# A perceiver layer on one core: tile 0 of the experts tied to expert 0, its weights fetched and split in earlier stages

## What is computed

```python
gout = x @ Wgate + bgate                      # 1024 tokens, 8 experts
topv, topi = jax.lax.top_k(gout, 2)
topw = jax.nn.softmax(topv, axis=-1)
x1 = x @ W1[e] + b1[e];  x2 = x @ W2[e] + b2[e];  z = x1 * x2
g = z @ Wg[e] + bg[e]
o = g * sigmoid(g) * (z @ Wl[e] + bl[e])
y = o @ W3[e] + b3[e]                         # summed over the token's two experts with topw
```

## Time and profile before

| | us |
|---|---|
| median of 3 runs (lowest, highest) | 2017.91 (2017.11, 2163.83) |
| profiled execution | 2020.24 |
| its span, first to last instruction | 2018.5 |
| mean granted TensorE clock, share of full speed | 0.961 |
| TensorE busy | 1843.3 (91%) |
| VectorE busy | 1601.7 (79%) |
| ScalarE busy | 1225.7 (61%) |

### The profile page before, as it was taken

The page is one execution under the profiler, slowest core; times in us unless marked ns, Lnnn a source line. Parts: engine busy times, 40 slices in busy tenths (PEclk is TensorE's granted clock), DMA queues, the critical chain, the costliest instruction groups (busy, mean ns, idle before and its releaser), DMA issues. The chain is left out here.

```text
span 2018.5 us, 33904 instructions
## 1 busy us (share of the span) xinstructions
PE 1843.3 (91%) x10010; PEld 1513.9 (75%) x10010; DVE 1601.7 (79%) x2790; ACT 1225.7 (61%) x2259; POOL 559.9 (28%) x388
## 2 busy tenths in 40 slices
PE   5978999999999999999999999999698756999995
PEld 4757777777777777777777777777485446999994
DVE  6758888898798988988889889878574856888863
ACT  3436666666676666766766767666452425777751
POOL 3022423334234232342342423412003731000003
PEclk9989999999999999999999999999798977999996
DMA  4621111111111111111111111010552026666632
GB/s 157 269 74 36 40 49 56 40 40 47 53 47 38 38 57 48 43 42 58 45 38 40 55 48 46 22 32 11 197 199 99 1 100 214 210 214 204 219 119 73
DMA packets 158260, 172.49 MB, mean 85 GB/s; under 512 B 13528, under 2 KB 124912, under 8 KB 158192
## 3 DMA queue, kind: packets, MB, share of 16 engines
q1 hardware_dynamic: 156656, 167.44, 25.6%
q0 software_dynamic: 1536, 4.20, 0.6%
HBM read 127.04 MB, written 44.56 MB: 85 GB/s over the span
## 5 line engine op out<-in xcount | busy, mean ns | idle before, releaser
L590 POOL TENSOR_TENSOR cl<-nrm,ch 128x255 fp32r<-128x255 f32 (+1 forms) x208 | 308.8, 1487 | 577.0 <-DVE ch L762 577.0
L688 ACT ACTIVATE s<-score 128x512 f32<-128x512 f32 (+1 forms) x416 | 248.4, 597 | 352.2 <-PE score L127 352.1
L721 DVE TENSOR_TENSOR s<-s,most 128x512 f32<-128x512 f32 (+1 forms) x416 | 321.9, 774 | 69.4 <-ACT most L664 69.4
L727 DVE TENSOR_TENSOR pl<-s,ph 128x512 fp32r<-128x512 f32 (+1 forms) x416 | 357.7, 860 | 0.7 <-ACT ph L670 0.7
L125 PE MATMUL acc<-ph,cl 128*128 128x512 f32 (+1 forms) x832 | 342.3, 411 | 1.4 <-DVE pl L727 1.4
L125 PE MATMUL score<-qsh,tl 128*128 128x512 f32 (+1 forms) x832 | 339.0, 407 | 0.8 <-DVE tl L756 0.8
L127 PE MATMUL score<-qsh,th 128*128 128x512 f32 (+1 forms) x832 | 326.7, 393 | 0.0
L126 PE MATMUL score<-qsl,th 128*128 128x512 f32 (+1 forms) x832 | 326.6, 393 | 0.0
L127 PE MATMUL acc<-ph,ch 128*128 128x512 f32 (+1 forms) x832 | 326.0, 392 | 0.0
L126 PE MATMUL acc<-pl,ch 128*128 128x512 f32 (+1 forms) x832 | 325.6, 391 | 0.0
L739 DVE TENSOR_TENSOR top<-top,s 128x512 f32<-128x512 f32 (+1 forms) x352 | 250.2, 711 | 19.4 <-ACT s L688 19.3
(11 more groups left out here) (257 smaller groups left out, 3456.6 us busy)
## 6 DMA issues: line engine op xcount, KB each, us to landing
raw<-in_ctx_in SPq DMA_DIRECT2D x192, 128.0 KB, 2.0
wr<-in_W SPq DMA_DIRECT2D x45, 512.0 KB, 4.8
queries_scratch<-stage SPq DMA_DIRECT2D x32, 512.0 KB, 3.5
qr<-queries_scratch SPq DMA_DIRECT2D x64, 256.0 KB, 3.3
outputs_scratch<-o SPq DMA_DIRECT2D x64, 256.0 KB, 2.4
at<-outputs_scratch SPq DMA_DIRECT2D x16, 1024.0 KB, 7.6
wr<-in_Wg SPq DMA_DIRECT2D x15, 1024.0 KB, 7.1
wr<-in_Wl SPq DMA_DIRECT2D x15, 1024.0 KB, 5.7
```

The costliest lines, as they stand in the source:

```text
L590: pool.tensor_tensor(cl[0:rows(t), t, 1:DIM], nrm[0:rows(t), t, 1:DIM], ch[0:rows(t), t, 1:DIM].bitcast(F32), ALU.subtract).then_inc(r_low, 1)
L688: act.activation(s[0:n, u, t, :], score[0:n, slot(0, u, t) % 2, :], ACT.Copy).then_inc(copied, 1)
L721: v.tensor_tensor(s[0:n, u, t, :], s[0:n, u, t, :], most[0:n, u, :], ALU.subtract).then_inc(shifted, 1)
L727: v.tensor_tensor(pl[0:n, ring(t), :], s[0:n, u, t, :], ph[0:n, ring(t), :].bitcast(F32), ALU.subtract).then_inc(p_low, 1)
```

## The change

Tile 0 is owned by expert 0 always: in `over`, the comparison for the first tile of expert 0 is with -1 instead of 0, so that it has a tile even with no tokens. With this its weights are known ahead of routing. A new class `Weights` holds the buffers and semaphores, and `load`, `high` and `low`. SP loads expert 0's weights at the end of its queue in `self_attention`. In `route`, ACT does `high` of all four parts first, and VectorE `low` of parts 0 and 1 behind the normalisation; parts 2 and 3 follow in `experts`. ACT and VectorE also split `xn` into `xnh` and `xnl` in `route`, which lie in the buffers `zh` and `zl`. The one-hot steps multiply these two parts in single passes into separate banks of `pp`, whose sums are copied as `xh` and `xl` without another subtraction. In `experts`, SP issues biases and weights of tile 1 ahead of the wait for `sent`. TensorE's order is `products(0)`, `gate(0)`, `first(1)`, and then steps from 0 with `gate(0)` left out. `y` lies in `xn` now, and `o` has a buffer of its own.

```diff
@@ self_attention, SP
                     sp.dma_start(flat[:, n * w4:(n + 1) * w4], nil[:, :]).then_inc(cleared, 16)
+                for n in range(4):
+                    ew.load(sp, *We, n, 0)
                 sp.wait_ge(cleared, 64)
@@ class Weights
+    def high(self, act, i, b, n):
+        act.wait_ge(self.w_in[n], (32 if n == 0 else 16) * (i + 1))
+        act.activation(self.wh[:, b, self.parts[n]], self.wr[:, self.parts[n]], ACT.Copy).then_inc(self.w_high[n], 1)
+
+    def low(self, v, i, b, n):
+        v.wait_ge(self.w_high[n], i + 1)
+        v.tensor_tensor(self.wl[:, b, self.parts[n]], self.wr[:, self.parts[n]],
+                        self.wh[:, b, self.parts[n]].bitcast(F32), ALU.subtract).then_inc(self.w_low[n], 1)
@@ route, ACT
+                for n in range(4):
+                    ew.high(act, 0, 0, n)
                 ln.scalar_copy(act)
+                act.activation(xnh[:, :, :], xn[:, :, :], ACT.Copy).then_inc(x_parts, 1)
@@ route, VectorE
                 ln.vector_normalise(v)
+                ew.low(v, 0, 0, 0)
+                ew.low(v, 0, 0, 1)
+                v.wait_ge(x_parts, 1)
+                v.tensor_tensor(xnl[:, :, :], xn[:, :, :], xnh[:, :, :].bitcast(F32), ALU.subtract
+                                ).then_inc(x_parted, 1)
...
-                for n in range(4):
+                inc(v.tensor_scalar(over[:, 0, 0:1], rank[:, TT, 0:1], -1.0, None, ALU.is_gt))
+                inc(v.tensor_scalar(over[:, 0, 1:], rank[:, TT, 1:], 0.0, None, ALU.is_gt))
+                for n in range(1, 4):
@@ experts, SP
-                e0 = expert(0)
+                first_biases(0, 0, 0)
+                gate_biases(0, 0, 0)
+                e1 = expert(1)
+                first_biases(1, 1, e1)
                 for n in range(4):
-                    weights(0, n, e0)
-                first_biases(0, 0, e0)
+                    weights(1, n, e1)
+                tile_rows(1, 1)
                 tiles(sp, step)
@@ experts, GpSimd
+                halves(0, 0, 0)
                 tiles(pool, step)
@@ experts, TensorE
+                pe.wait_ge(x_parted, 1)
                 for i in range(TT):
                     pe.wait_ge(hot_made, i + 1)
                     for c in range(DC):
-                        m = pe.matmul((pt, py)[c][:, 0, :], xn[:, i, c * P:(c + 1) * P], u[:, i % 2, :],
-                                      start=i == 0, stop=i == TT - 1)
+                        for n, w in enumerate((xnh, xnl)):
+                            m = pe.matmul(pp[:, 2 * c + n, 0, :], w[:, i, c * P:(c + 1) * P], hot_r[:, i % 2, :],
+                                          start=i == 0, stop=i == TT - 1)
                     m.then_inc(hot_used if i < TT - 1 else turned, 1)
+                pe.wait_ge(x_taken, 2)
+                products(0, 0)
+                gate(0, 0)
+                first(1, 1, 0)
                 tiles(pe, step)
@@ experts, ACT
-                high(0, 0, 0)
                 act.wait_ge(turned, 1)
-                act.activation(xh[:, 0, :], pt[:, 0, :], ACT.Copy).then_inc(x_half, 1)
-                act.activation(xh[:, 1, :], py[:, 0, :], ACT.Copy).then_inc(x_high, 1)
-                for n in range(1, 4):
-                    high(0, 0, n)
+                for c in range(DC):
+                    m = act.activation(xh[:, c, :], pp[:, 2 * c, 0, :], ACT.Copy)
+                m.then_inc(x_high, 1)
+                act.wait_ge(x_high, 1)
+                act.nop().then_inc(x_taken, 1)
+                x1_parts(0, 0, 0)
+                high_z(0, 0, 1)
+                high(1, 1, 0)
+                high(1, 1, 1)
+                gates(0, 0)
+                first(1)
                 tiles(act, step)
```

More of the change, by code:

```diff
@@ L1560, in weights @@
                 def weights(i, n, e):
[L1561 to L1567, removed]
+                    sp.wait_ge(w_low[n], i)
+                    ew.load(sp, *We, n, e)
                 def step(i, b, h):
@@ L1596, in _, with halves, step @@
                 pool.wait_ge(point5_made, 1)
+                def halves(i, b, h):
+                    if not on(i):
+                        return
+                    pool.wait_ge(bg_in[b], 16 * (h + 1))
+                    wait(pool, tanh_done, FC * (i - 1))
+                    pool.tensor_tensor(halfg[:, b], bias[:, b, 2 * FC:3 * FC], point5[:, :], ALU.mult
+                                       ).then_inc(b_half, 1)
+                def step(i, b, h):
+                    halves(i + 1, 1 - b, h if b == 0 else h + 1)
                 for i in range(TT):
@@ new lines, in gates @@
+                def gates(i, b):
+                    if not on(i):
+                        return
+                    for f in range(FC):
+                        act.wait_ge(g_made, FC * i + f + 1)
+                        if f == 0:
+                            act.wait_ge(b_half, i + 1)
+                        wait(act, u_done, FC * i + f - 1)
+                        act.activation(tanh[:, f % 2, :], pp[:, f, 0, :], ACT.Tanh, scale=0.5,
+                                       bias=halfg[:, b, f:f + 1]).then_inc(tanh_done, 1)
+                        act.activation(g[:, f % 2, :], pp[:, f, 0, :], ACT.Identity,
+                                       bias=bias[:, b, 2 * FC + f:2 * FC + f + 1]).then_inc(g_done, 1)
+                        if f == 2:
+                            high_o(i, 0)
@@ L1827, in step @@
                     low(i + 1, 1 - b, 2)
+                    low_z(i + 1, 1 - b, 1)
                     first(i + 2)
-                    low_z(i + 1, 1 - b, 1)
                     low(i + 2, b, 0)
                     low(i + 1, 1 - b, 3)
-                    if isinstance(i, int) and i == 0:
-                        v.wait_ge(sent, 16 * TT * TOP)
-                    for f in range(FC):
-                        gated(i, b, f)
-                        if f == 2:
-                            low_o(i, 0)
+                    if not isinstance(i, int) or i > 0:
+                        for f in range(FC):
+                            gated(i, b, f)
+                            if f == 2:
+                                low_o(i, 0)
@@ new lines, in _ @@
+                low(0, 0, 2)
+                v.wait_ge(turned, 1)
+                for c in range(DC):
+                    m = v.tensor_copy(xl[:, c, :], pp[:, 2 * c + 1, 0, :])
+                m.then_inc(x_low, 1)
+                v.wait_ge(x_low, 1)
+                v.nop().then_inc(x_taken, 1)
+                low(0, 0, 3)
+                for f in range(FC):
+                    product(0, 0, f)
+                    if f == 2:
+                        low_z(0, 0, 0)
+                low_z(0, 0, 1)
@@ L1852, in _ @@
+                low(1, 1, 0)
+                for f in range(FC):
+                    gated(0, 0, f)
+                    if f == 2:
+                        low_o(0, 0)
+                first(1)
                 tiles(v, step)
```

161 lines of the change are left out of this document (81 added, 80 removed).

## The result

The changed kernel takes 2028.73 us (median of 5 runs, 2028.1 to 2030.62) against 2020.59 us (5 runs) for the kernel before beside it on the same chip: ratio 1.0046, interval 1.0028 to 1.0064. One run of before took 2163.83 us in a slow state and is left out of the ratio; without it the median is 2019.25. The change costs some 9 us, by the interval 6 to 13; forecast were 7.7 us less. The profiled execution took 2030.62 us and spans 2028.9.

A forecast was written before the change was run, and what follows sets the result against it. TensorE runs expert tiles back to back from 1694 us, so only the stretch ahead can shrink: 9.0 us won at `products(2)`, less 1.3 for clock, gives 7.7 us and 2010.2 us; 8-in-10 range 2005 to 2015.5.

The forecast's parts named there:

- The step that failed: From the start of `products(2)` on: same matmul queue in both kernels, so the gain there lasts to the end.
- Clock: Experts' start: half-rate matmuls cost 1.3 us ahead of `products(0)` and 1.3 ahead of `products(2)`, nothing ahead of gate 0.
- the forecast's chain: Experts' start without clock losses: `products(0)` at 1658.8, gate 0 at 1667.15, `products(1)` at 1680.8, `products(2)` at 1694.6 us.
- What is late next: Ahead of `products(2)`: VectorE's 11.6 us chain sets its start 13.75 us after `products(1)`, TensorE idle some 8 us.
- Self-attention and route: Expert 0's weight fetch hidden, cost nothing; extra splits in route make it 0.2 us later, bounds 0 and 0.8.
- First rows in two parts: One-hot steps on split `xn`: `products(0)` starts at 1658.8 instead of 1660.83 us, gain 2.0, bounds 1.2 and 2.6.
- Arithmetic: Figures of 19.5 us idle time going, and of tile 1's rows landing at 1680.6 with scatters 2.4 later.
- The first (GpSimd held up): Scatters ahead of tile 1's rows: VectorE's two-input operations end them 2.4 us later, giving 2011.2 us; chance 0.12.
- The third (only the start is won, 2 to 4 us): Ahead of `products(2)`: `low` chain some 5 us longer, tile 2's transfer behind `sent` on SP; 2014 to 2016 us; chance 0.1.
- The slower case: Experts' start: scatters end so late that `x_in` and `b_half` come after the covered 11 us; 2020.5 us; chance 0.03.

The follow-up runs named there:

- e5: Changed kernel with 320 unused bytes ahead of the split weights and 192 behind them; 2015.66 us, ratio 0.9981 to the kernel before.
- e10: As e5, with 4, 6, 4 and 15 unread constant matmuls in TensorE's waits of the experts' start; 2010.97 us, 0.9954 to the kernel before.
- e13: Changed kernel with its own addresses, plus only the added constant matmuls of e10; 2024.15 us, ratio 1.0021 to the kernel before.
- e12: Changed kernel with 192 unused bytes behind the split weights; 2015.00 us, ratio 0.9975 to the kernel before.
- e2: Kernel before with 64 unused bytes ahead of `wh` and 64 behind `wl`; 2031.67 us, ratio 1.0054 to the unpadded kernel before.
- e3: Kernel before with 64 unused bytes behind `wl` alone; 2031.59 us, ratio 1.0057 to the unpadded kernel before.
- e1: Changed kernel with 64 unused bytes ahead of `wh` and 64 behind `wl`; 2022.59 us, ratio 1.0010 to the kernel before.
- e4: Changed kernel with 64 unused bytes behind `wl` alone; 2022.80 us, ratio 1.0006 to the kernel before.
- e7: As e5, plus pads of 64 bytes in the stages of queries, cross-attention and output projection; 2020.25 us, ratio 1.0001 to the kernel before.
- e9: As e5, plus 192 bytes ahead of the moving operands of cross-attention and its output projection; 2031.76 us, ratio 1.0063 to the kernel before.
- e11: As e5, but `gate(0)` back in its turn behind `products(1)` on all three engines; 2015.68 us, ratio 0.9985 to the kernel before.

## Why the prediction was wrong

Starts after that of `products(0)`, in us:

| | `gate(0)` | `products(1)` | `products(2)` | `gate(1)` |
|---|---|---|---|---|
| before | 33.1 | 25.8 | 44.1 | 52.6 |
| forecast for after | 8.4 | 22.0 | 35.8 | |
| after | 10.7 | 26.2 | 41.8 | 53.4 |
| e5 | 10.7 | 27.2 | 41.3 | 51.2 |
| e10 (clock kept) | 8.6 | 22.6 | 36.6 | 45.2 |

**The step that failed** is the sentence at the end of the first part: "From there both kernels have the same queue of matmuls, and what has been won at that point is won at the end, provided TensorE stays without a gap". It stayed without a gap and the queue is the same; its rate isn't. At `outputs(0)` the changed kernel was 1.5 us ahead, eleven tiles later 8.2 behind. By the ratios of after and e5 the term that I had at nothing is 0.0065 of the time, 13 us (by the two intervals, 9 to 18), of which 10 lie in the eleven tiles measured. It comes from the moved buffers, which stand in the diff and for which the forecast has no term. No wait, no busy share and no granted clock shows it.

**Clock.** I summed 1.3 ahead of `products(0)` and 1.3 ahead of `products(2)` and took the wait ahead of `gate(0)` as free. It wasn't (clock 0.62 from 1668 to 1671), nor was the 2.07 us ahead of `products(1)`, and the stretch from `products(2)` stayed at half rate until about 1706, 5.8 us and not 2.9. Keeping the clock gives 5 us by medians; at `gate(1)` it gives 6.0 with e5's addresses and 7.2 with the changed kernel's own (e13: 46.2). With it the forecast's chain, which stands in the table without its clock losses, holds to within 0.8 us at each of its three points. So the durations and their order in "What is late next" were right (a wait of 8 us, measured 7.7, ended by the last `low`), and the clock term was mis-sized: 2.6 forecast, 5 to 7 measured. The Trainium skill, "TensorE: Matmul & The Clock Gate", section "HAM oscillation — how this bites in real kernels", describes this: waits between short batches send the clock back each time, so that every batch starts slow. The trace of the kernel after agrees, for waits of 3.2 us and even 2.07; my forecast treated each wait by itself. In e5 the same wait of 2.07 us cost nothing, so the short one isn't a loss each time:

```profile
1688.00:1691.00 3.00, 3.00 (x27) 3.00 (x27) 0.96 (x2) 0.53 (x2) 0.00 (x0) 1.00 0.00 0
```

**Self-attention and route.** The issues for expert 0 hid, and `r_best` starts at 1636.65 us, against 1637.03 in the earlier trace rows. A shift of 0.2 us can't be told: in the other traces of the changed kernel that leave the stages ahead of `route` as they are, `r_best` starts anywhere from 1635.84 to 1638.98.

**First rows in two parts**: forecast 1658.8, measured 1658.64. That close a hit is luck, for the same reason; but from `r_best` to `products(0)` it is 22.0 us in after, e5, e10 and e12 alike, against 23.8 before, a gain of 1.8 as forecast.

**Arithmetic.** Two slips are in terms that the sum doesn't use: the idle time of the earlier trace rows is 18.8 us and not 19.5, and 1678.40 plus 2.4 is 1680.8, not 1680.6.

**Rivals.** The first (GpSimd held up) wasn't the cause: the last scatter starts at 1671.44 us, in the kernel before at 1671.36, and in e10 `products(1)` started at 22.6 us. The third (only the start is won, 2 to 4 us) is near the lead of 1.5 at `outputs(0)`, but for another reason than SP's queue: 3.0 of the 4.5 us won at `products(2)` are lost up to `outputs(0)`, most of them to the half rate. The slower case had a chance of 0.03 and a mechanism that didn't occur; a change of TensorE's own rate was in none of the rivals.

The two failed terms account for nearly all of the miss, within what the intervals allow: from the forecast's ratio of 0.9962 to 1.0046 are 0.0084, 17 us; 13 are the addresses and 3 the clock beyond its forecast 2.6. Without either loss the forecast would have been 10.3 us of gain, 0.9949; e10, which has neither, measured 0.9954.

## What to carry to other kernels

When a change allocates, moves or resizes buffers, compare the addresses of the matmuls' operands before and after, and read the distance of matmul starts in a stretch without waits: it showed up to 6% here where busy share, durations and clock showed nothing. Put the pad in by trial, for each column count apart, and undo the placing before judging the rest of a change. When work is moved into a wait of TensorE, take as the bad case that every batch behind a wait like those here (2.07, 3.2 and 7.7 us) starts at half rate, and see whether constant matmuls in the wait win it back.

## What the hardware showed unexpectedly

- Starts of `fp32r` matmuls of 256 columns stand 120.0 ns apart at full clock when stationary and moving operand lie at the same place modulo 256 bytes (after, e2, e3; 128 bytes apart wasn't tried); 117.8 or 113.3 at other distances, 116.7 and 118.3 at 32 bytes. Modulo 256, weights 64 bytes above the activations gave the most of 113.3 (before, e5, e12), 64 below mostly 117.8 (e1, e4). The output projection, in which the weights are the moving operand, says that the roles count: 113 ns in e7, 117.8 in e9. `outputs` has the same roles and agrees in e1 (114.0), but in before, e5 and e12 it has 113.4 where these roles would give 117.8; why is open. With 512 columns the order is another: 227 at the same place, 229 in e7 and 233 in e9. What in the chip does this wasn't found.
- Where two levels occur, a level starts at a turn and holds for a whole stretch. The pattern is mostly one stretch in four in before and e5, two in three in e11, none in e12 until `gate(13)`. Why is open. It may also be why before spreads over 2014.5 to 2029.3 us where kernels at 120.0 ns spread over some 3, but e12, without it in its one traced execution, spreads over 11.
- The granted clock can fall after TensorE has resumed: `products(1)` of the kernel after starts at full rate after 2.07 us of waiting, falls to half within 1 us and stays there for 3 us, while it works without a gap.
